# Products with the values of the first attention in four column parts of the array, denominators summed on GpSimd

## The reference

```
xn = layernorm(x, ln_x_g, ln_x_b)            # 77 context rows
ln = layernorm(latents, ln_l_g, ln_l_b)      # 1024 rows per batch element
q = ln @ Wq.T
kv = concatenate([xn @ Wkv.T, ln @ Wlkv.T])  # 77 + 1024 keys and values
qn = rmsnorm(q, qn_g) * SCALE
kn = rmsnorm(k, kn_g)
attn = softmax(where(mask, qn @ kn.T, -max))
out = (attn @ v) @ Wo.T + bo                 # 4 heads of 64, then x + out
```

## Time and profile before

| | before |
|---|---|
| median of 3 runs | 883.65 us (881.67 to 890.49) |
| the profiled execution | 877.26 us |
| its span in the profile | 875.3 us |
| PE, DVE, ACT, POOL busy over the span | 89%, 63%, 45%, 35% |
| granted TensorE clock, mean | 0.978 |
| first attention, first to last exponential | 62.1 to 370.0 us |

### The profile page before, as it was taken

The page is one execution under the profiler, slowest core; times in us unless marked ns, Lnnn a source line. Parts: engine busy times, 40 slices in busy tenths (PEclk is TensorE's granted clock), DMA queues, the critical chain, the costliest instruction groups (busy, mean ns, idle before and its releaser), DMA issues.

```text
span 875.3 us, 13078 instructions
## 1 busy us (share of the span) xinstructions
PE 782.6 (89%) x4960; PEld 634.2 (72%) x4960; DVE 548.9 (63%) x1219; ACT 396.1 (45%) x721; POOL 307.2 (35%) x289
## 2 busy tenths in 40 slices
PE   3779988999999999989989989887489999999996
PEld 3666554656665555577968979886379999999996
DVE  6677786667587585255543469894846556565552
ACT  3434543454445434455271244443117655566561
POOL 5413001200120013036362123433425576676773
PEclk9999999999999999999999999997699999999999
DMA  7000000000000010010003020112212354343522
GB/s 180 1 1 1 0 1 2 1 0 1 1 1 1 1 51 1 0 49 3 1 1 92 1 97 1 49 50 96 75 48 73 86 145 133 82 135 88 145 32 31
DMA packets 20111, 38.41 MB, mean 44 GB/s; under 512 B 4507, under 2 KB 15633, under 8 KB 17745
## 3 DMA queue, kind: packets, MB, share of 16 engines
q1 hardware_dynamic: 13393, 29.14, 10.1%
q0 software_dynamic: 6656, 8.43, 5.5%
HBM read 29.02 MB, written 8.40 MB: 43 GB/s over the span
## 4 chain that ended last, share of the span: by engine, by line
PE 58%; DVE 15%; ACT 4%; issue 4%; POOL 2%; DMA 0%; DVEq 0%; ACTq 0%; POOLq 0%
PE ps L453 18%; PE ps L1086 11%; PE ps L593 8%; PE ps L693 6%; PE ps L610 2%; PE ps L611 2%; PE ps L555 2%; DVE sm L1459 1%; ACT htmp L1958 1%; DVE rep L1647 1%; DVE Pb L1463 1%; PE ps L1026 1%; PE ps L1014 1%; DVE mxp L1254 1%; DVE sm L1468 1%
## 5 line engine op out<-in xcount | busy, mean ns | idle before, releaser
L593 PE MATMUL ps<-PT,VA 128*65 128x512 f32 (+1 forms) x288 | 147.2, 593 | 0.3 <-ACT PT L1900 0.2
L1900 ACT ACTIVATE PT<-ps 128x512 f32<-128x512 f32 x128 | 76.0, 595 | 62.2 <-PE ps L611 61.7
L1086 PE MATMUL ps<-he,wh 128*128 128x258 f32 x768 | 104.0, 288 | 0.0
L453 PE MATMUL ps<-GT,wh 128*128 128x258 f32 x768 | 99.0, 286 | 2.4 <-ACT het L2176 1.9
L453 PEld LDWEIGHTS ps<-GT,wh 128*128 128x128 f32 x768 | 94.0, 189 | 4.5 <-ACT het L2176 4.0
L1086 PEld LDWEIGHTS ps<-he,wh 128*128 128x128 f32 x768 | 95.4, 189 | 0.4
L1766 DVE TENSOR_TENSOR he<-het,he 128x516 fp32r<-128x516 f32 x64 | 44.6, 696 | 48.2 <-ACT he L1794 37.5
L2486 POOL DMA_INDIRECT out_dram<-ye,idx x40 | 66.9, 1672 | 22.5 <-DVE ye L1748 12.0
L2228 POOL TENSOR_TENSOR rs<-rs,half 128x4 f32<-128x4 f32 (+2 forms) x19 | 17.8, 938 | 156.7 <-DVE rs L1126 127.6
L2237 POOL TENSOR_TENSOR ssq<-ssq,half 128x4 f32<-128x4 f32 x32 | 32.3, 1008 | 115.6 <-DVE ssq L1198 115.4
L610 PE MATMUL ps<-QA,KA 128*128 128x512 f32 x144 | 68.3, 474 | 1.6 <-DMA QB<-mrt 1.6
(11 more groups left out here) (267 smaller groups left out, 1583.3 us busy)
## 6 DMA issues: line engine op xcount, KB each, us to landing
wr<-in_w1e_dram SPq DMA_DIRECT2D x8, 1024.0 KB, 4.9
wr<-in_w2e_dram SPq DMA_DIRECT2D x8, 1024.0 KB
x<-in_x_dram SPq DMA_DIRECT2D x4, 512.0 KB, 6.9
w<-in_w_dram SPq DMA_DIRECT2D x2, 1024.0 KB, 4.7
y_dram<-yr SPq DMA_DIRECT2D x3, 512.0 KB, 3.0
out_dram<-x SPq DMA_DIRECT2D x3, 512.0 KB, 4.4
gt<-y_dram,idx POOLq DMA_INDIRECT x40
out_dram<-ye,idx POOLq DMA_INDIRECT x40
```

Source lines behind the costliest of these rows:

```text
L453: op = pe.matmul(o, l, r, start=n == 0, stop=n == len(calls) - 1)
L593: pe.matmul(bank[6 + hf][0:65, :], VA[b][0:K, kt, h, :], PT[u % 4][0:K, :], start=kt == 0, stop=kt == 8).then_inc(p_pv, 1)
L1086: op = pe.matmul(bank[dc][:, 0:258], w2h[i][:, wc_], he[j][:, m, 258 * c:258 * c + 258], start=n == 0, stop=n == 23)
L1900: a.activation(PT[u % 4][0:K, :], bank[4 + u % 2][0:K, :], ACT.Exp, bias=0.0 if K == 128 else mcol[:, b:b + 1]).then_inc(a_exp, 1)
```

## The change

Products with values. The 64 columns of values are taken as two pieces of 32. A product writes 32 partitions of the result and uses 32 of the array's columns: units of even number partitions 0 to 31 and 32 to 63, units of odd number 64 to 95 and 96 to 127. So bank 6 or 7 holds two partial sums over the tiles of keys, one above the other, which the output product adds up, since both halves of wo now hold the same Wo rows (128 rows in place of 65, 256 columns in place of 258). PE no longer makes the product of one unit per unit: after the scores of units 5, 9, 13 and 17 it makes those of four units in a row, and the last two after unit 1 of the next head. PT has eight tiles in place of four. The context keys come first in a half in place of last (`KEYS`).

Denominators. There is no column of ones. GpSimd adds the nine tiles PT of a half in pairs to four tiles PS (five additions, line 2388 and 2391 of the new kernel). PE multiplies the four with 32 columns of ones, each in its own part (`sums`), ACT copies the bank to dn, PE turns it (`sums_turned`, four transpositions), DVE adds the four parts and takes the reciprocal for four tiles of queries at once (`denominators`). The bias bo is added to x by GpSimd (`add_bias`) in place of the row in wo.

Around them: the copy of a half into OT and its row of maxima come later (units 2 and 14 in place of the half's end); `max_tile` and `wo_tile` stand behind other units (`MAX_AT`, `WO_AT`); QA, QB, KA and KB have three slots; the second bank of the side work is 6 in units 0 to 3 and 16 and 17, 7 in units 8 to 11, and otherwise 3, which is the first bank too. The last two units, `sums` and `sums_turned` of the last half stand among the products of the dense network. The core of the diff:

```diff
-MAX_AT = (4, 6, 7, 9, 10, 12, 13, 15)
+MAX_AT = ((4, 6, 7, 9, 10, 12, 15, 16), (0, 2, 4, 6, 8, 10, 12, 16))
+
+WO_AT = (1, 3, 5, 7, 9, 11, 15, 17)
+
+KEYS = (8, 0, 1, 2, 3, 4, 5, 6, 7)
+
+SUM_OF = (1, 0, 0, 2, 2, 3, 3, 4, 4)
+
+NPT, NPS = 8, 5
...
+def second_bank(u):
+
+    return 6 if u < 4 or u > 15 else 7 if 8 <= u < 12 else 3
...
-        wo = [RA(f"wo{i}", [65, H0, 258], F32R)[:, :, :] for i in range(2)]
+
+        wo = [RA(f"wo{i}", [128, H0, D], F32R)[:, :, :] for i in range(2)]
         qa_at = RA.at
-        QA = RA("QA", [128, H0, S], F32R)
-        QB = RA("QB", [65, H0, S], F32R)
-        KA = RA("KA", [128, H0, NK], F32R)
-        KB = RA("KB", [65, H0, NK], F32R)
-        VA = [RA(f"VA{i}", [128, 9, H0, 65]) for i in range(2)]
+
+        QA = RA("QA", [128, 3, S], F32R)
+        QB = RA("QB", [65, 3, S], F32R)
+        KA = RA("KA", [128, 3, NK], F32R)
+        KB = RA("KB", [65, 3, NK], F32R)
+        VA = [RA(f"VA{i}", [128, 9, H0, DH]) for i in range(2)]
...
+            def values(n):
+
+                hi, u = divmod(n, 18)
+                b, h = HEADS[hi]
+                hf, k = divmod(u, 9)
+                kt, K = KEYS[k], 128 if k else SC
+                if k == 0:
+                    clear(6 + hf)
+                pe.wait_ge(a_exp, n + 1)
+                if u == 0 and h == 0:
+                    pe.wait_ge(a_v, 8 * b + 8)
+                    pe.wait_ge(a_vc, b + 1)
+                for c in (0, 32):
+                    o = 64 * (u % 2) + c
+                    op = pe.matmul(bank[6 + hf][o:o + 32, :], VA[b][0:K, kt, h, c:c + 32], PT[n % NPT][0:K, :], start=k < 2, stop=k >= 7)
+                op.then_inc(p_pv, 1)
+                if k == 8:
+                    busy[6 + hf] = (v_ot, 2 * hi + hf + 1)
+
+            def sums(hi, hf):
+
+                H, m = 2 * hi + hf, 2 if hf == 0 or hi == 7 else 7
+                clear(m)
+                pe.wait_ge(g_sum, 5 * H + 5)
+                for j in range(4):
+                    op = pe.matmul(bank[m][32 * j:32 * j + 32, :], ones32[:, :], PS[(4 * H + j) % NPS][:, :], start=True, stop=True)
+                op.then_inc(p_den, 1)
+                busy[m] = (a_den, H + 1)
+
+            def sums_turned(hi, hf):
+                H, m = 2 * hi + hf, 0 if hf == 0 else 2 if hi == 7 else 7
+                clear(m)
+                pe.wait_ge(a_den, H + 1)
+                for t in range(4):
+                    op = pe.transpose(bank[m][:, 128 * t:128 * t + 128], dn[:, 128 * t:128 * t + 128], ident[:, :])
+                op.then_inc(p_dT, 1)
+                busy[m] = (v_den, H + 1)
+
             def attention(hi):
-                b, h = HEADS[hi]
-                units = [(hf, kt) for hf in range(2) for kt in range(9)]
-
-                def pv(u):
-                    hf, kt = units[u]
-                    K = 128 if kt < 8 else SC
-                    if kt == 0:
-                        clear(6 + hf)
-                    pe.wait_ge(a_exp, 18 * hi + u + 1)
-                    if hf == 0 and kt == 0 and h == 0:
-                        pe.wait_ge(a_v, 8 * b + 8)
-                        pe.wait_ge(a_vc, b + 1)
-                    pe.matmul(bank[6 + hf][0:65, :], VA[b][0:K, kt, h, :], PT[u % 4][0:K, :], start=kt == 0,
-                              stop=kt == 8).then_inc(p_pv, 1)
-                    if kt == 8:
-                        busy[6 + hf] = (v_ot, 2 * hi + hf + 1)
-
+                h = hi % 3
                 if hi == 0:
-                    pe.wait_ge(g_init, 6)
-                for u, (hf, kt) in enumerate(units):
+                    pe.wait_ge(g_init, 5)
+                for u in range(18):
                     at["unit"] = u
-                    K = 128 if kt < 8 else SC
+                    hf, k = divmod(u, 9)
+                    kt, K = KEYS[k], 128 if k else SC
                     ks, qc = slice(128 * kt, 128 * kt + K), slice(512 * hf, 512 * hf + 512)
                     m = 4 + u % 2
                     clear(m)
                     if u == 0:
                         pe.wait_ge(v_ka, 2 * hi + 2)
-                    if kt == 0:
+                    if k == 0:
                         pe.wait_ge(d_mrow[2 * (hi % 2) + hf], 16 * (hi // 2 + 1))
                     pe.matmul(bank[m][0:K, :], KA[:, h, ks], QA[:, h, qc], start=True, stop=False)
                     pe.matmul(bank[m][0:K, :], KB[:, h, ks], QB[:, h, qc], start=False, stop=True).then_inc(p_s, 1)
                     busy[m] = (a_exp, 18 * hi + u + 1)
-                    if u:
-                        pv(u - 1)
+
+                    if u == 1 and hi:
+                        values(18 * hi - 2)
+                        values(18 * hi - 1)
+                        max_row(hi, 1)
+                    if u in (5, 9, 13, 17):
+                        for w in range(u - 5, u - 1):
+                            values(18 * hi + w)
+                    if u == 5 and hi:
+                        sums(hi - 1, 1)
+                    if u == 13:
+                        sums(hi, 0)
+                    if hi == 0 and u == 6:
+                        max_row(0, 1)
+                    if hi < 7 and u == (11 if hi == 0 else 9):
+                        max_row(hi + 1, 0)
+                    if u == 7 and hi:
+                        sums_turned(hi - 1, 1)
+                    if u == 15:
+                        sums_turned(hi, 0)
                     if hi == 0 and u < 4:
                         max_tile(0, 4 + u)
-                    if hi == 0 and u == 6:
-                        max_row(0, 1)
-                    when = MAX_AT if hi == 0 else range(0, 16, 2)
+                    when = MAX_AT[min(hi, 1)]
                     if hi < 7 and u in when:
                         max_tile(hi + 1, when.index(u))
-                    if hi < 7 and u == (11 if hi == 0 else 9):
-                        max_row(hi + 1, 0)
-                    if hi < 7 and u == 17:
-                        max_row(hi + 1, 1)
-                    if hi and u % 2 and u < 16:
-                        wo_tile(hi - 1, u // 2)
-                    yield
-                pv(17)
+                    if hi and u in WO_AT:
...
+            def denominators(hi, hf):
+
+                H, m = 2 * hi + hf, 0 if hf == 0 else 2 if hi == 7 else 7
+                v.wait_ge(p_dT, H + 1)
+                step(v.tensor_reduce(den[:, :], bank[m].rearrange("p (t j c) -> p t j c", t=4, j=4)[:, :, :, 0], AX.X, ALU.add))
+                settle()
+                v.reciprocal(rec[:, 4 * hf:4 * hf + 4], den[:, :]).then_inc(v_den, 1)
...
+                    if hi and u == 6:
+                        denominators(hi - 1, 1)
+                    if u == 14:
+                        denominators(hi, 0)
                     a.wait_ge(p_s, n + 1)
-                    if n >= 4:
-                        a.wait_ge(p_pv, n - 3)
-                    a.activation(PT[u % 4][0:K, :], bank[4 + u % 2][0:K, :], ACT.Exp,
+                    if n >= NPT:
+
+                        hn, k = divmod(n - NPT, 9)
+                        a.wait_ge(p_pv, n - NPT + 1)
+                        a.wait_ge(g_sum, 5 * hn + SUM_OF[k] + 1)
+                    a.activation(PT[n % NPT][0:K, :], bank[4 + u % 2][0:K, :], ACT.Exp,
                                  bias=0.0 if K == 128 else mcol[:, b:b + 1]).then_inc(a_exp, 1)
...
+            def attention(hi):
+
+                for u in range(18):
+                    hf, k = divmod(u, 9)
+                    if k and k % 2 == 0:
+                        n, H = 18 * hi + u, 2 * hi + hf
+                        i = 4 * H + k // 2 - 1
+                        s_ = PS[i % NPS][:, :]
+                        if i >= NPS:
+                            g_.wait_ge(p_den, (i - NPS) // 4 + 1)
+                        g_.wait_ge(a_exp, n + 1)
+                        g_.tensor_tensor(s_, PT[(n - 1) % NPT][:, :], PT[n % NPT][:, :], ALU.add).then_inc(g_sum, 1)
+                        if k == 2:
+                            g_.wait_ge(g_sum, 5 * H + 1)
+                            g_.tensor_tensor(s_[0:SC, :], s_[0:SC, :], PT[(n - 2) % NPT][0:SC, :], ALU.add).then_inc(g_sum, 1)
```

243 lines of the change are left out of this document (156 added, 87 removed).

## The result

The changed kernel takes 933.99 us in the median (929.63 to 937.29), beside 884.1 us for the kernel before on the same chip: ratio 1.055, interval 1.048 to 1.062. It is slower by 50 us where I had forecast 16 us less. A second measurement gave 1.0576 (1.0544 to 1.0607). The time lies inside the range (838 to 948), but by luck: the range's upper end stood for products two abreast, and that is not what happened.

What follows compares the result with a forecast made beforehand. PE's stream was taken to bound the first attention (291.9 of 307.9 us). Terms -63.4 + 14.1 + 6.4 + 4 + 9 + 10 + 4 = -16 us gave 867 us from the median 883.65; whole range 838 to 948 us.

Steps and rivals of the forecast that it cites:

- products two abreast: Rival: only a second half and the following product's first half overlap on PE; 942 us, chance 0.24.
- Values four abreast: PE's products with values: four column parts run side by side, 0.44 us per unit, -63.4 us.
- sums: PE's four products with ones per half of a head, four abreast at 0.88 us: +14.1 us.
- turning: PE's four transpositions of the denominators' sums per half of a head, 0.10 us each: +6.4 us.
- the changes in and out: PE going into column parts and out again, 40 groups at 0.1 us each: +4 us, upper bound 12.
- Both rivals: PE's parts overlap only two abreast (942 us, chance 0.24) or run one after another (1077 us, chance 0.08).
- one side bank: Side work in bank 3 alone in units 4-7 and 12-15 waits for emptying: +9 us, bounds 0 and 40.
- the cover of bank 2: Maxima's tile waits for DVE's addition to x in units without side work: +10 us, bounds 0 and 25.
- at nothing, the row of maxima: Fetching the row of maxima later was taken as hidden by PE's stream: 0 us.
- GpSimd at 4 us: GpSimd's additions are hidden but delay roots that DVE's large multiplication waits for: +4 us, at most 8.
- PE's share of the stage over 85%: Sign for the profile after: PE's busy share in the first attention should stay over 85%.
- DVE's time coming near the stage's length: Sign of being wrong: DVE's busy time in the first attention comes near that stage's length.

Runs made afterwards that it cites:

- the order mended: Changed kernel with values two units at a time, row of maxima copied a unit earlier, GpSimd's norm and weight work in heads seven and eight spread over later units: 1.0406.
- the kernel before with 18 waits: Kernel before, plus PE waiting in units 4, 8 and 12 of heads two to seven until DVE has reduced the tile of maxima: ratio 1.0288.
- pairs: Changed kernel with products with values two units at a time in every odd unit, behind the output tile, not four at a time: ratio 1.0562.
- the moved row: Changed kernel with ACT copying the second half's row of maxima in unit 1 and not unit 2: ratio 1.0579.
- without the denominators' path: Kernel with pairs, the moved row and the order mended, without additions, sums, turning, copies and reductions for denominators (a constant instead): ratio 0.9897.

## Why the prediction was wrong

The sum had -39 us of work, 23 us of waits (9 + 10 + 4) and nothing for the clock. The stage shows -25, +46 and +30. So what failed is that what leaves PE's stream comes off the time: the condition which the prediction set for it, that no other wait takes its place, did not hold at three of its terms, and the clock fell behind the waits.

**Right: the products.** Values four abreast (62.6 us against 63.4 predicted as what is left), sums (15.5 against 14.1), turning (6.6 us for 60 of the 64 transpositions, against 6.4), and the changes in and out (the 560 halves in the stage take 65.3 us, by the count used below, and 60.9 at the group's price: 4.4 against 4). Both rivals in which the parts don't run side by side are out. **Right: one side bank**, 9 us predicted, 8.5 measured alone.

**Mis-sized: the cover of bank 2.** I counted 10 us in three heads' worth of units. The tile of maxima waits 16.3 us for x in the changed kernel, 13.7 of them in eleven waits of 0.6 to 2.2 us. The step that failed is "in a unit without side work the next maxima would be due 0.47 us after the output product": I gave the term to the units without side work and let the side work cover the others; but DVE has part of the side work to do before it comes to x, and the low part of the output, which the new order puts ahead of it, so a unit with side work waits too (1.52 us in the rows above).

**Wrong: at nothing, the row of maxima.** I put its later fetching at nothing, as hidden under PE's stream, with ACT idle for half of the stage. But the copy empties bank 0 for the next tile of maxima, and ACT's order puts it behind an exponential and an output copy: 9.4 us. The two waits stood one behind the other, so that each move alone gained nothing, and together they gained about 10 us (1.0576 to 1.0461).

**Wrong: GpSimd at 4 us.** I priced the queue on GpSimd, and called the additions hidden since GpSimd was idle. Their length costs 14 us in the changed kernel and 22 with the order mended, and 20 us in the kernel before together with GpSimd's changed order: DVE's work beside them takes longer, and where it doesn't meet them GpSimd's roots come later. How the price divides between the two stays open. The late sums of the seventh and eighth head are in part in the 14 us; GpSimd's mended order gained 5 to 6. Here a rule was to be had that I had not weighed: the Trainium skill's page "SBUF — State Buffer", section "SBUF: two separate sides", says that DVE and GpSimd share one pair of ports, and that the one that comes second stands still for the whole instruction of the other, where DVE's instruction has two inputs in SBUF or runs in a mode with two ports. The runs agree: a row of centring beside an addition of 1.27 us took 1.35 us, the multiplication with two inputs in SBUF went from 2284 ns to 2554, and what reads PSUM kept its length (search for maxima 914 and 916 ns, addition to x 484 and 475).

**Absent from the sum: the clock.** Every term was priced at the clock of the earlier trace rows. Idle time of PE brought it to 1.2 GHz in 72 us of the stage, which cost some 30 us, more than the whole gain in work. The price of a wait in this stage was thus 1.65 times its length: 46 us of idle time and 30 us of clock. In the kernel before with 18 waits it was about 1.5 (17.6 us of idle time, 8 of clock: 16 us of busy time in its two stretches at half the clock).

**Absent: the work behind a wait.** PE's work fell by 25 us, not by 39 (-63.4 + 14.1 + 6.4 + 4). Each product is counted here from the end of the one ahead of it (or from its own start behind a wait) to its own end, at the granted clock. Then the tiles of maxima take 41.7 us where they took 34.4, and the output products 23.4 where they took 20.6. A product of maxima that starts behind a wait (over 0.06 us) counts 0.42 us, one that follows another product mostly 0.17 to 0.20; 43 of them start behind a wait in the changed kernel and 13 in the kernel before. Where the waits go, this work goes: with pairs, the moved row, the mended order and additions one column wide 17 start behind a wait (35.7 us), and without the denominators' path 13 again (34.8 us).

The sum in one line: -25 us of work, +46 us of idle time and +30 us of clock make the stage's 50.5 us. One sign that I had named, PE's share of the stage over 85%, came out at 83% (296.17 of 358.4), with most of the missing share in line 583. The other sign, DVE's time coming near the stage's length, did not show: 215 of 358 us. DVE was late, not full.

Left open: whether products in parts let the clock fall more readily than full ones, how the price of the additions divides between slower rows on DVE and later roots on GpSimd, and how much of the idle time the waits on bank 3 take in the changed kernel itself.

## What to carry to other kernels

When PE is the bound with 95% of its stage, a product that becomes shorter also stops hiding hand-overs, and the order in which DVE and ACT empty banks has to be priced at the new length before the gain is. Price a wait of PE with the clock behind it, and price an addition on an idle engine by what its neighbours do beside it and by what queues behind it. When a move of one wait gains nothing, look for the next wait in the same place before dropping it.
